# A residual block in one pipeline: the late order from body 3 on, and other PSUM banks

## The chip, the cores and the metric

The kernel runs on one core of a Trainium2 chip. The metric is the device time of one execution in microseconds (us); the table below has the median of three runs.

## What is computed

```python
def _L0_ffn_ref(x, Win, bin_, W1, b1, W2, b2, Wout, bout):
    s = jnp.einsum('btd,dm->btm', x, Win) + bin_
    h = jax.nn.relu(s[..., None] * W1 + b1)
    g = jnp.einsum('btmh,mh->btm', h, W2) + b2
    out = jnp.einsum('btm,md->btd', g, Wout) + bout
    return out
x = L0_attn_x                 # (4, 4096, 512), fp32
xn = _layernorm(x, axis=-1)
x = x + _L0_attn_ref(xn, ...) + _L0_ffn_ref(xn, ...)
```

The feed-forward part has 64 inner columns (M) with 16 hidden units each. The attention part runs only over 16 tokens of each of the 4 batches: it is three rounds of a small attention (a local linear map, layer norms, logits, softmax, product with the values) whose result picks, by a threshold, the output of the second or the third round, followed by Wo. Its result is added to those 64 rows of the output, all others get the bias bo alone.

## The kernel before, in words

The 16,384 rows of x are cut into 16 **pairs** (bodies) of 1,024 rows, two halves of 512. Each row is 2 KB, so a body loads 2.1 MB (`load`, `load_pair`) and stores as much; the second half is also read a second time in 32-row pieces (`load_quads`, 0.5 MB for each half of it, buffers `xq`, 1 MB a body), because VectorE turns it by stream transposes. That is 5.24 MB of DMA a body. For body n the steps are:

- TensorE turns the first half of x (`transpose` or `transpose_late`, into PSUM), ScalarE copies it out (`evacuate`, `evacuate_late`); VectorE turns the second half (`turn_quads`).
- VectorE takes statistics (`statistics`, eight of them, and `variance`), GpSimd makes 1/std (`inv_std`), TensorE spreads it over columns (`spread_rstd`, `spread_late`), ScalarE copies that into `s_full` (`copy_rstd`).
- TensorE multiplies by Win (`s_product`), VectorE scales (`scale_s`), and s is split into a high and a low part (`s_high` on ScalarE, `s_low` on VectorE).
- TensorE replicates s to the 1,024 hidden rows in two halves (`replicate`, banks `rep`), ScalarE does eight activations (`relu`), TensorE sums them with W2 in four steps (`sum_h`), ScalarE copies g out (`evacuate_g`), and TensorE multiplies by Wout in four pieces (`project`). VectorE adds each piece to x in place (`add`), GpSimd adds the bias (`add_bias`, eight), and SyncE stores.

Three bodies are in work at once: in iteration n of the main loops stand the first steps of body n, `replicate`, `sum_h` and the hidden activations of bodies n-1 and n-2, and `project` and `add` of body n-3. Every engine runs a program of its own, written out in order, with semaphores between them, and nothing reorders it. There are two loops. For n below LATE (10) the turned half goes through one bank in four groups of 128x128 tiles, each copied by 512 columns. From LATE on, `transpose_late` turns by 64x64 tiles into both TA banks, two chunks of columns, each copied by 1,024, and `s_product_late` uses 128x32 tiles. The loop below LATE has places (`reach(side, n, k)`) at which the attention's steps are slipped in; where each goes is set by the tables AT_PE, AT_ACT, AT_DVE and AT_POOL (32 n + place). In the loop from LATE on there are none, and the attention has to be over by then, since it works in the second TA bank (`A_ps`).

TensorE is used in tile shapes (rows x columns of the array): 128x128, 128x64, 128x32, 64x128 and 64x64. In the trace `project` is L628 (64x128), `replicate` L572 (64x128), `sum_h` L590 (128x32), `transpose` L474 (128x128), `transpose_late` and `spread_late` L482 (64x64), `s_product` L542 (128x64), `s_product_late` L518 (128x32). L329 (`product_qk`) and L356 are of the attention's setup: L356 turns the four weight matrices and ScalarE and VectorE (L997) copy them out; L329 waits for the copies of Wq and Wk.

The work of SyncE's queue at the start is one list of loads: x of bodies 0 and 1, biases, Wq, Wk, x of body 2, Wv, Wo, the quads of body 2, Wout and some 18 small loads, then x of body 3, for whose place Wq and Wk must have been turned.

## Time and profile before

| | us |
|---|---|
| median of 3 runs (lowest to highest) | 321.81 (321.6 to 322.66) |
| the profiled execution itself | 323.47 |
| its span | 321.7 |
| TensorE busy | 287.7 (89%) |
| VectorE busy | 251.5 (78%) |
| GpSimd busy | 236.5 (74%) |
| ScalarE busy | 232.8 (72%) |
| packets of SyncE's queue, share of 16 DMA engines | 67.3% |
| packets of ScalarE's queue, share of 16 DMA engines | 18.5% |

The span is what the trace shows from the first to the last instruction; 1.8 us of the profiled execution lie around it. An engine's busy time is a union over stages with different limits: read it by stretch. Every fp32 matmul stands in the trace as two records, and records of matmuls that run side by side in different tiles, or one behind the other in the pipeline, overlap; what a step costs TensorE is the distance from its first record to the first record of the next step.

### The profile page before, as it was taken

The numbers are of one execution on the slowest core, as the hardware profiler recorded it, in microseconds if no ns is written. First come the engines' busy times: TensorE is split into PE (matmuls) and PEld (weight loads), VectorE is DVE, ScalarE is ACT, GpSimd is POOL, SyncE is SP. The second block draws the span as 40 slices with busy tenths as digits, with TensorE's granted clock in tenths as the row PEclk, the third lists the DMA queues.
The fourth block names the chain that finished last, engine by engine and source line by source line (L and its number), as shares of the span: only waits on it lengthen the run. The fifth ranks groups of instructions, "written<-read, shape, count | busy, mean of one in ns | idle before, by whom it ended". The sixth has DMA issues, their size and how long they took to land.

```text
span 321.7 us, 5598 instructions
## 1 busy us (share of the span) xinstructions
PE 287.7 (89%) x2035; PEld 128.7 (40%) x2035; DVE 251.5 (78%) x400; ACT 232.8 (72%) x296; POOL 236.5 (74%) x209
## 2 busy tenths in 40 slices
PE   4878769989989999999999979899987999999882
PEld 3645514544533544345443424334332444342220
DVE  0769455679689787897889999999996899976444
ACT  1448624685896879987698776888868789898840
POOL 8440995781892989829895694598989498999960
PEclk9999969999999999999999999999997999999998
DMA  7999939996429979698996989899999999632697
GB/s 230 293 368 407 264 52 317 384 268 202 154 72 336 287 239 349 180 334 244 340 281 212 339 229 342 243 341 291 300 331 341 378 333 341 236 154 109 242 284 276
DMA packets 50571, 87.83 MB, mean 273 GB/s; under 512 B 6360, under 2 KB 35184, under 8 KB 46448
## 3 DMA queue, kind: packets, MB, share of 16 engines
q1 hardware_dynamic: 46400, 65.96, 67.3%
q10 hardware_dynamic: 3504, 21.37, 18.5%
q0 software_dynamic: 640, 0.16, 0.8%
q8 instruction: 16, 0.26, 0.4%
q14 instruction: 11, 0.09, 0.1%
HBM read 53.77 MB, written 33.69 MB: 272 GB/s over the span
## 4 chain that ended last, share of the span: by engine, by line
PE 45%; DVE 25%; SPq 9%; issue 8%; DMA 7%; ACT 2%; POOL 2%; ACTq 0%; DVEq 0%; POOLq 0%
PE op L628 9%; PE sg L590 9%; DVE x L1099 8%; DVE stats L1126 5%; PE sg L518 5%; SPq L245 4%; PE sg L542 4%; DMA out_dram<-x 4%; DMA xq<-in_L_attn_x_dram 3%; DVE xqT L1109 3%; PE rep L572 3%; SPq L264 3%; DVE SL L1120 3%; PE TA L329 2%; PE TA L474 2%
## 5 line engine op out<-in xcount | busy, mean ns | idle before, releaser
L1245 POOL TENSOR_TENSOR x<-x,bias_row 128x512 f32<-128x512 f32 x128 | 162.4, 1313 | 0.0
L840 ACT ACTIVATE H<-rep,b1c,w1c 128x1024 f32<-128x1024 f32 x124 | 143.7, 1219 | 18.2 <-PE rep L572 16.3
L1126 DVE BATCH_NORM_STATS2 stats<-x 128x6 f32<-128x512 f32 x128 | 79.7, 676 | 9.6 <-DMA x<-in_L_attn_x_dram 9.6
L1099 DVE TENSOR_TENSOR x<-x,op 128x1024 f32<-128x1024 f32 x53 | 64.3, 1213 | 19.8 <-PE op L628 19.7
L1229 POOL TENSOR_TENSOR rstd<-veps,nhalf 128x8 f32<-128x8 f32 x16 | 26.7, 1672 | 53.9 <-DVE veps L1136 53.9
L590 PE MATMUL sg<-H,w2s 128*32 128x512 f32 x512 | 64.2, 606 | 0.0
L628 PE MATMUL op<-wout,G 64*128 64x512 f32 x212 | 57.8, 622 | 4.9 <-DVE x L1099 4.1
L1109 DVE STREAM_TRANSPOSE xqT<-xq 128x1024 f32<-128x1024 f32 x28 | 34.6, 1235 | 10.1 <-PE sg L542 6.3
L542 PE MATMUL sg<-xT,win 128*64 128x512 f32 x80 | 36.4, 598 | 1.6 <-ACT xqT L804 1.6
L804 ACT ACTIVATE xT<-TA 128x512 f32<-128x512 f32 x40 | 24.0, 607 | 14.9 <-PE TA L474 14.8
L474 PE MATMUL TA<-ident,x 128*128 128x128 f32 x192 | 30.2, 290 | 3.9 <-DMA x<-in_L_attn_x_dram 2.6
L542 PE MATMUL sg<-xqT,winq 128*64 128x512 f32 x64 | 29.2, 598 | 0.0
L474 PEld LDWEIGHTS TA<-ident,x 128*128 128x128 f32 x192 | 22.2, 147 | 16.6 <-issue 9.6
L590 PEld LDWEIGHTS sg<-H,w2s 128*32 128x32 f32 x512 | 13.2, 108 | 33.6 <-issue 21.5
L628 PEld LDWEIGHTS op<-wout,G 64*128 64x128 f32 x212 | 17.3, 185 | 18.7 <-issue 10.5
L518 PE MATMUL sg<-xT,win 128*32 128x512 f32 x96 | 22.6, 614 | 0.0
L518 PE MATMUL sg<-xqT,winq 128*32 128x512 f32 x96 | 22.6, 614 | 0.0
L572 PE MATMUL rep<-SH,spread 64*128 64x512 f32 x62 | 17.9, 572 | 2.4 <-DVE SL L1120 2.3
L542 PEld LDWEIGHTS sg<-xT,win 128*64 128x64 f32 x80 | 10.1, 136 | 23.5 <-issue 23.5
L1231 POOL TENSOR_TENSOR rwide<-rstd,ones_d 128x512 f32<-128x512 f32 x16 | 17.0, 1062 | 1.3
L1114 DVE TENSOR_TENSOR s_full<-sg,s_full 128x512 f32<-128x512 f32 x16 | 10.8, 678 | 7.1 <-PE sg L518 7.1
L1120 DVE TENSOR_TENSOR SL<-s_full,SH 128x512 fp32r<-128x512 f32 x16 | 14.5, 908 | 1.8 <-ACT SH L826 1.8
(189 smaller groups left out, 363.0 us busy)
## 6 DMA issues: line engine op xcount, KB each, us to landing
out_dram<-x SPq DMA_DIRECT2D x30, 1024.0 KB, 6.0
x<-in_L_attn_x_dram ACTq DMA_DIRECT2D x10, 2048.0 KB, 11.2
xq<-in_L_attn_x_dram SPq DMA_DIRECT2D x112, 128.0 KB, 8.6
x<-in_L_attn_x_dram SPq DMA_DIRECT2D x12, 1024.0 KB, 12.2
out_dram<-x SPq DMA_DIRECT2D x4, 512.0 KB, 3.4
x<-in_L_attn_Wq_dram SPq DMA_DIRECT2D x1, 1024.0 KB, 18.8
x<-in_L_attn_Wk_dram SPq DMA_DIRECT2D x1, 1024.0 KB, 21.0
x<-in_L_attn_Wv_dram SPq DMA_DIRECT2D x1, 1024.0 KB, 16.1
```

The source lines that it names most:

```text
L474: mm = pe.transpose(bank(n, g)[:, j::TILES], x_sb[m][:, col0:col0 + P], ident[:, :])
L518: mm = pe.matmul(own, w[:, c, a * MH:(a + 1) * MH], turned_x, start=(c == 0), stop=(c == DC - 1))
L542: mm = pe.matmul(own, w[:, c, :], turned_x, start=(c == 0), stop=(c == DC - 1))
L572: mm = pe.matmul(rep_banks(n, half)[:, b * BLK:(b + 1) * BLK], spread[own, half, :], part[own, :], start=(part is SH), stop=(part is SL), ...
L590: mm = pe.matmul(g_ps[at0:at0 + MH, :], w2s[:, half, k, :], Hr[half][k % len(Hr[half])][:, b * BLK:(b + 1) * BLK], start=(k == 0), stop=(k ...
L628: mm = pe.matmul(sum_banks(n, j)[:, b * D:(b + 1) * D], G[n % 2][own, j * P:(j + 1) * P], wout[own, :], start=True, stop=True, tile_positi ...
L840: act.activation(Hr[half][k % len(Hr[half])][:, :], rep_banks(n, half)[:, :], ACT.Relu, bias=b1c[:, half, k:k + 1], scale=w1c[:, half, k:k ...
L1099: dve.tensor_tensor(both, both, sum_banks(n, j)[:, :].rearrange("p (h d) -> p h d", h=2), ALU.add).then_inc(add_done, 1)
L1109: dve.transpose(xqT[:, h * QH:(h + 1) * QH, :, :].rearrange("p t c a -> p (t c a)"), xq[k % 3][:, :]).then_inc(tq_done, 1)
L1126: dve.bn_stats(stats[:, j, :], x_sb[m][:, j * D:(j + 1) * D]).then_inc(bn_done, 1)
L1229: pool.tensor_tensor(rstd[:, :], veps[:, :], nhalf[:, 0:TPP], ALU.pow).then_inc(rstd_done, 1)
L1245: pool.tensor_tensor(x_sb[m][:, c], x_sb[m][:, c], bias_row[:, :], ALU.add).then_inc(xc_done, 1)
```

## The change

The second shape of the loop now serves bodies 3 to 15 (LATE is 3), in a new order on TensorE, ScalarE and VectorE, and has places for the attention. The eight PSUM banks are dealt anew: the attention gets a bank (`A`), g gets one, and s shares the second TA bank with the transposes, `spread_late` and piece 1 of `project`, which needs both. So of body n, TA holds in turn: s(n-1), piece 1 of body n-3, the two chunks of x, the spread, s(n). All eight statistics of a body are taken in the body before. The quads of body 2 are loaded ahead of Wv and Wo. The last bodies' order (the tail) is new. The tables of places are new from body 3 on, and equal ahead of it but for VectorE's statistics. Left out of the diff are the tables, the waits of `replicate` and `project` that follow from the banks, and `turn_halves`, which takes its target as an argument.

```diff
-        TA_ps, sg_ps, o_ps, rep_ps = ps("TA", 2), ps("sg", 2), ps("op", 2), ps("rep", 2)
-        T_ps, A_ps = TA_ps[:, 0:BLK], TA_ps[:, BLK:2 * BLK]
-        s_ps, g_ps = sg_ps[:, 0:BLK], sg_ps[:, BLK:2 * BLK]
+        TA_ps, g_ps, A_ps, o_ps, rep_ps = ps("TA", 2), ps("g"), ps("A"), ps("op", 2), ps("rep", 2)
...
-        LATE = 10
+        LATE = 3
...
         def early(n):
 
-            return 2 if n < LATE - 2 else min(TPP, 2 * (n - LATE + 4))
+            return 2 if n < LATE else TPP
...
             load_weight(1, Wk)
             load(2, 0)
             load(2, 1)
+            load_quads(0)
+            load_quads(1)
             load_weight(2, Wv)
             load_weight(3, Wo)
-            load_quads(0)
-            load_quads(1)
...
             if i == 0:
                 pe.wait_ge(*(landed(n, 0)))
-                pe.wait_ge(R_done, n)
-                if n == LATE:
-                    pe.wait_ge(att_made, 1)
+                pe.wait_ge(add_done, TILES * (n - 3) + 2)
...
         def s_product_late(n):
 
-            pe.wait_ge(s_done, n)
-            pe.wait_ge(ev_done, groups(n + 1))
+            pe.wait_ge(R_done, n + 1)
             pe.wait_ge(tq_done, 2 * (n + 1 - BY_PE))
...
-                if LATE - 3 < n < N - 2:
-                    pe.wait_ge(add_done, TILES * (n - 1) + 2)
...
         def sum_banks(n, j):
 
-            if LATE - 3 <= n < N - 3 and j == 1:
-                return sg_ps
-            if (n, j) in ((N - 3, 1), (N - 2, 1), (N - 2, 3), (LAST, 2)):
+            if n < N - 3 and j == 1:
                 return TA_ps
-            return rep_ps if (n, j) == (LAST, 1) else o_ps
+            if (n, j) in ((N - 2, 1), (N - 2, 3), (LAST, 2)):
+                return TA_ps
...
             for n in range(LATE, N):
+                replicate(n - 2, 1)
+                reach(side, n, 0)
                 project(n - 3, 0)
-                replicate(n - 2, 1)
+                reach(side, n, 1)
                 project(n - 3, 1)
+                reach(side, n, 2)
+                sum_h(n - 2, 0)
+                reach(side, n, 3)
+                sum_h(n - 2, 1)
+                reach(side, n, 4)
+                project(n - 3, 2)
+                reach(side, n, 5)
                 transpose_late(n, 0)
-                project(n - 3, 2)
-                sum_h(n - 2, 0)
-                sum_h(n - 2, 1)
+                reach(side, n, 6)
+                replicate(n - 1, 0)
+                reach(side, n, 7)
+                transpose_late(n, 1)
+                reach(side, n, 8)
+                project(n - 3, 3)
+                reach(side, n, 9)
+                spread_late(n)
+                reach(side, n, 10)
                 sum_h(n - 2, 2)
-                transpose_late(n, 1)
-                replicate(n - 1, 0)
-                project(n - 3, 3)
-                spread_late(n)
+                reach(side, n, 11)
                 sum_h(n - 2, 3)
+                reach(side, n, 12)
                 s_product_late(n)
+                reach(side, n, 13)
             replicate(N - 2, 1)
             project(N - 3, 0)
+            sum_h(N - 2, 0)
             project(N - 3, 1)
-            sum_h(N - 2, 0)
+            replicate(LAST, 0)
+            sum_h(N - 2, 1)
+            sum_h(N - 2, 2)
             project(N - 3, 2)
-            sum_h(N - 2, 1)
-            replicate(LAST, 0)
-            sum_h(N - 2, 2)
             sum_h(N - 2, 3)
-            replicate(LAST, 1)
             project(N - 3, 3)
             project(N - 2, 0)
+            replicate(LAST, 1)
             project(N - 2, 1)
+            project(N - 2, 2)
             sum_h(LAST, 0)
-            project(N - 2, 2)
+            project(N - 2, 3)
             sum_h(LAST, 1)
-            project(N - 2, 3)
             sum_h(LAST, 2)
             sum_h(LAST, 3)
...
             for n in range(LATE, N):
                 relu(n - 2, 4)
+                reach(side, n, 0)
                 relu(n - 2, 5)
+                reach(side, n, 1)
+                s_high(n - 1)
+                reach(side, n, 2)
                 relu(n - 2, 6)
-                s_high(n - 1)
+                reach(side, n, 3)
+                relu(n - 2, 7)
+                reach(side, n, 4)
                 evacuate_late(n, 0)
-                relu(n - 2, 7)
-                if has(n + AHEAD):
+                reach(side, n, 5)
+                relu(n - 1, 0)
+                reach(side, n, 6)
+                evacuate_late(n, 1)
+                if n + AHEAD >= RING and has(n + AHEAD):
                     load_pair(n + AHEAD)
-                evacuate_late(n, 1)
-                relu(n - 1, 0)
+                reach(side, n, 7)
+                relu(n - 1, 1)
+                reach(side, n, 8)
                 copy_rstd_late(n)
-                relu(n - 1, 1)
+                reach(side, n, 9)
+                relu(n - 1, 2)
+                reach(side, n, 10)
+                relu(n - 1, 3)
+                reach(side, n, 11)
                 evacuate_g(n - 2)
-                relu(n - 1, 2)
-                relu(n - 1, 3)
+                reach(side, n, 12)
             relu(N - 2, 4)
             s_high(LAST)
             relu(N - 2, 5)
             relu(N - 2, 6)
             relu(N - 2, 7)
             relu(LAST, 0)
+            relu(LAST, 1)
             evacuate_g(N - 2)
-            for r in range(1, TPP):
+            for r in range(2, TPP):
                 relu(LAST, r)
...
             for n in range(LATE, N):
                 scale_s(n - 1)
+                reach(side, n, 0)
+                variance(n)
+                reach(side, n, 1)
+                turn_quads(n, 0)
+                reach(side, n, 2)
                 add(n - 3, 0)
+                reach(side, n, 3)
                 add(n - 3, 1)
-                variance(n)
+                reach(side, n, 4)
+                s_low(n - 1)
+                reach(side, n, 5)
                 add(n - 3, 2)
-                turn_quads(n, 0)
-                s_low(n - 1)
+                reach(side, n, 6)
                 turn_quads(n, 1)
+                reach(side, n, 7)
+                add(n - 3, 3)
+                reach(side, n, 8)
                 if has(n + 1):
-                    statistics(n + 1, 0)
-                add(n - 3, 3)
-                if has(n + 1):
-                    for j in range(1, TPP):
+                    for j in range(TPP):
                         statistics(n + 1, j)
+                        reach(side, n, 9 + j)
```

What this does to the order is shown at three places. The names: `rep` is the replicated s, `H` the hidden activations, `G` the summed g, `SH` and `SL` the parts of s, `op`, `sg`, `g`, `TA` and `A` are PSUM banks, `x` and `xT` the rows and their transpose, `xq` the quads. Line numbers differ between the two kernels: L572, L590, L628, L482 and L518 are L566, L582, L619, L481 and L514 in the changed one.

TensorE, one body of the late shape (n = 13), from behind one `s_product_late` on, before:

```order
L628 MATMUL op<-wout,G 128x512 x2
L572 MATMUL rep<-SH,spread 128x512 x2
L572 MATMUL rep<-SL,spread 128x512 x2
L628 MATMUL sg<-wout,G 128x512 x2
L482 MATMUL TA<-ident,x 128x64 x16
L628 MATMUL op<-wout,G 128x512 x2
L590 MATMUL sg<-H,w2s 32x512 x12
L482 MATMUL TA<-ident,x 128x64 x16
L572 MATMUL rep<-SH,spread 128x512 x2
L572 MATMUL rep<-SL,spread 128x512 x2
L628 MATMUL op<-wout,G 128x512 x2
L482 MATMUL TA<-ident,rwide 128x64 x8
```

and now:

```order
L566 MATMUL rep<-SH,spread 128x512 x2
L566 MATMUL rep<-SL,spread 128x512 x2
L619 MATMUL op<-wout,G 128x512 x2
L619 MATMUL TA<-wout,G 128x512 x2
L582 MATMUL g<-H,w2s 32x512 x8
L619 MATMUL op<-wout,G 128x512 x2
L481 MATMUL TA<-ident,x 128x64 x16
L566 MATMUL rep<-SH,spread 128x512 x2
L566 MATMUL rep<-SL,spread 128x512 x2
L481 MATMUL TA<-ident,x 128x64 x16
L619 MATMUL op<-wout,G 128x512 x2
L481 MATMUL TA<-ident,rwide 128x64 x8
```

Two of the four `sum_h` of the body (x8 for x12) now stand ahead of the first transposes, and the two others behind the spread; `replicate` of the new body stands between the two chunks of transposes.

TensorE in the middle of the attention (L419 and L427 before, L401 to L418 now, are steps of its second round). Before, body 6:

```order
L419 MATMUL TA<-ident,vn 128x128 x4
L474 MATMUL TA<-ident,x 128x128 x4
L628 MATMUL op<-wout,G 128x512 x2
L572 MATMUL rep<-SH,spread 128x512 x2
L572 MATMUL rep<-SL,spread 128x512 x2
L474 MATMUL TA<-ident,x 128x128 x4
L550 MATMUL sg<-ident,rwide 128x128 x4
L427 MATMUL TA<-WvT,qk 64x256 x4
L628 MATMUL op<-wout,G 128x512 x2
L590 MATMUL sg<-H,w2s 32x512 x4
L474 MATMUL TA<-ident,x 128x128 x4
L628 MATMUL op<-wout,G 128x512 x2
```

and now, body 5, from its first chunk of transposes:

```order
L481 MATMUL TA<-ident,x 128x64 x16
L401 MATMUL A<-kT,bd 128x256
L402 MATMUL A<-vT,bd 128x256
L566 MATMUL rep<-SH,spread 128x512 x2
L566 MATMUL rep<-SL,spread 128x512 x2
L407 MATMUL A<-avg,vn 128x4 x4
L481 MATMUL TA<-ident,x 128x64 x16
L619 MATMUL op<-wout,G 128x512 x2
L412 MATMUL A<-ident,vT 128x128 x4
L481 MATMUL TA<-ident,rwide 128x64 x8
L582 MATMUL g<-H,w2s 32x512 x8
L418 MATMUL A<-ident,vn 128x128 x4
```

Four steps of a round stand in one body, between steps of other tile shapes, and the last of them (L418) directly ahead of the product with Win.

SyncE's queue at the start, before:

```order
L245 DMA x<-in_L_attn_x_dram 128x2048 x2
L267 DMA x<-in_L_attn_Wv_dram 128x4x512
L267 DMA x<-in_L_attn_Wo_dram 128x4x512
L264 DMA xq<-in_L_attn_x_dram 32x8x128 x8
L295 DMA wout<-in_L_ffn_Wout_dram 64x512
```

and now:

```order
L244 DMA x<-in_L_attn_x_dram 128x2048 x2
L263 DMA xq<-in_L_attn_x_dram 32x8x128 x8
L266 DMA x<-in_L_attn_Wv_dram 128x4x512
L266 DMA x<-in_L_attn_Wo_dram 128x4x512
L294 DMA wout<-in_L_ffn_Wout_dram 64x512
```

The eight quad loads of body 2 (1 MB) went ahead of Wv and Wo (2.1 MB).

## Rows read from the trace of the kernel before

**Rows 1.** Chain that ended last, 25 to 66 us (start, us, engine and line).
```profile
30.78 10.28 DMA xq<-in_L_attn_x_dram
...
42.96 6.67 PE TA L329 x16
```

**Rows 2.** VectorE in order of time, before L329.
```profile
41.09 1.25 DVE L1109 STREAM_TRANSPOSE xqT<-xq 128x1024 f32<-128x1024 f32 x1 [3.73 <-DMA xq<-in_L_attn_x_dram]
```

**Rows 3.** By stretch: us; busy PE, PEld, DVE, ACT, POOL; clock; DMA share; GB/s.
```profile
38.90:42.96 4.06, 0.05 (x1) 0.00 (x0) 1.87 (x3) 3.41 (x5) 4.06 (x5) 0.91 0.80 158
42.96:49.60 6.64, 6.64 (x17) 1.75 (x17) 2.29 (x3) 0.00 (x0) 6.64 (x6) 0.54 0.31 31
49.60:62.00 12.40, 12.40 (x100) 6.69 (x100) 8.61 (x20) 6.69 (x12) 6.60 (x6) 1.00 1.05 364
62.00:213.70 151.70, 144.51 (x950) 64.28 (x952) 131.49 (x211) 122.01 (x168) 110.77 (x85) 1.00 0.87 263
122.40:139.56 17.16, 16.78 (x106) 6.91 (x105) 14.54 (x20) 15.78 (x24) 13.28 (x11) 1.00 0.85 252
122.40:159.88 37.48, 36.84 (x239) 16.52 (x237) 31.62 (x49) 31.48 (x46) 29.18 (x23) 1.00 0.91 281
213.70:227.70 14.00, 13.61 (x132) 5.54 (x128) 13.86 (x21) 12.44 (x14) 13.04 (x11) 1.00 1.06 303
227.70:245.06 17.36, 14.57 (x133) 5.58 (x129) 17.22 (x27) 12.79 (x14) 16.43 (x14) 0.96 1.06 328
213.70:288.00 74.30, 69.93 (x648) 28.27 (x644) 69.10 (x100) 62.15 (x66) 65.34 (x51) 0.98 0.95 308
```

**Rows 4.** TensorE in order of time, body 6, four-group shape with attention.
```profile
126.00 0.66 PE L419 MATMUL TA<-ident,vn 128*128 128x128 f32 x4
126.50 0.60 PE L474 MATMUL TA<-ident,x 128*128 128x128 f32 x4
...
130.03 1.08 PE L427 MATMUL TA<-WvT,qk 128*64 128x256 f32 x8 [0.38 <-DVE qk L1057]
131.04 1.13 PE L628 MATMUL op<-wout,G 64*128 64x512 f32 x4
```

**Rows 5.** TensorE in order of time, body 11, late shape.
```profile
219.68 0.66 PE L482 MATMUL TA<-ident,x 64*128 64x64 f32 x16
220.18 1.08 PE L628 MATMUL op<-wout,G 64*128 64x512 f32 x4
221.27 2.78 PE L590 MATMUL sg<-H,w2s 128*32 128x512 f32 x24
...
225.07 0.49 PE L572 MATMUL rep<-SH,spread 64*128 64x512 f32 x2 [0.38 <-DVE SL L1120]
...
225.64 1.02 PE L628 MATMUL op<-wout,G 64*128 64x512 f32 x4
226.49 0.41 PE L482 MATMUL TA<-ident,rwide 64*128 64x64 f32 x8
226.83 1.07 PE L590 MATMUL sg<-H,w2s 128*32 128x512 f32 x8
...
231.26 1.13 PE L628 MATMUL op<-wout,G 64*128 64x512 f32 x4
```

**Rows 6.** ScalarE in order of time, body 11, late shape.
```profile
218.88 3.40 ACT L840 ACTIVATE H<-rep,b1c,w1c 128x1024 f32<-128x1024 f32 x3 [1.49 <-PE rep L572]
222.17 0.63 ACT L826 ACTIVATE SH<-s_full 128x512 fp32r<-128x512 f32 x1
222.69 1.02 ACT L815 ACTIVATE xT<-TA 128x1024 f32<-128x1024 f32 x1
```

**Rows 7.** DMA issues by kind (KB each, median us to landing).
```profile
x<-in_L_attn_x_dram SPq DMA_DIRECT2D x12, 1024.0 KB, 12.2
```

**Rows 8.** SyncE's queue in order of time, loads of body 3.
```profile
45.92 0.91 SPq L245 DMA_DIRECT2D x<-in_L_attn_x_dram  x2
```

**Rows 9.** Chain that ended last, 205 to 262 us, a store.
```profile
227.96 13.39 DMA out_dram<-x
```

45 lines of the change are left out of this document (22 added, 23 removed).

## The prediction

> **What bounds the kernel now.** I read the page's busy shares first, then busy time by stretch, then the chain that ended last, and for each place on which that chain rests the engine's instructions in order of time. Between the start of s(2) at 62.0 us and that of s(10) at 213.7 us, the eight bodies 3 to 10, TensorE is busy 144.51 of 151.70 us and no other engine over 131.5 [rows 3]; a pair of attention bodies takes 37.48 us with TensorE busy 36.84 [rows 3]. So TensorE's instruction stream sets the pace there. The five late bodies, 213.7 to 288.0, take 74.30 us with TensorE busy 69.93; an undisturbed one takes 14.00 us, with VectorE (13.86), GpSimd (13.04) and ScalarE (12.44) close behind, and the DMA engines full (share 1.06) [rows 3]. The start is another matter: the chain goes through the landing of the first quads (30.78 + 10.28 us) into L329, which takes 6.67 us [rows 1]; ahead of it TensorE did nothing for 4.06 us, and then worked at a granted clock of 0.54, near the lower of its two levels, 1.2 GHz [rows 3].
>
> **The start (quads ahead of Wv and Wo).** VectorE's queue stands behind the quads: it waits 3.73 us for them until 41.09 [rows 2], then copies the last turned part of Wk, and L329 waits for that copy. [...] At the 303 to 328 GB/s of full stretches [rows 3], 2.1 MB are over 6 us, more than the 3.73 us that VectorE waited. So L329 starts about 3.7 us sooner, and TensorE's gap of 4.06 us shrinks to some 0.3. The clock fell in that gap; without it the 6.64 us [rows 3] should shrink to half, 3.4, which gives 3.2 more. Bounds: 3.5 (the clock falls all the same) and 6.9. I take 6.9. From 49.6 to 62.0 TensorE is full, 12.40 of 12.40 us [rows 3], so all of it arrives. Against it: all eight statistics of body 3 now stand on VectorE ahead of the scaling of s(2). Body 3's x is issued at 45.92 [rows 8], and this kind lands 12.2 us later in the median [rows 7], so near 58; four statistics behind it end near 60, where s(2) would end at 58.7. I charge 1.0 us (bounds 0 and 3). **Start: -5.9.**
>
> **Bodies 3 to 10, TensorE's own work.** What does a body of the old shape cost without attention? Body 6 takes 17.16 us [rows 3]; off go L419, 0.50 us to the next step, and L427 with its wait, 0.38 + 1.01 [rows 4]. That leaves 15.27. A late body: 14.00 less the wait of 0.38 on SL [rows 3, 5] is 13.62. The new order has the same instructions. Its pieces, by start-to-start distances [rows 5]: `replicate` 0.57, `project` 0.85 where a 64x64 piece follows and 1.09 where `sum_h` does, `sum_h` 0.87 to 0.90, a chunk of transposes 0.50, the spread 0.34, s 3.56. In the new sequence: 0.66 + 0.85 + 1.09 + 1.90 + 0.95 + 0.50 + 0.57 + 0.50 + 0.85 + 0.34 + 1.77 + 3.56 = 13.5; I take 13.6. So each of bodies 3 to 9 loses 15.27 - 13.6 = 1.67 us of TensorE's work, 11.7 in all, and body 10 nothing. With the waits as long as now (151.70 - 144.51 = 7.2 us), bodies 3 to 10 would take 140.0.
>
> Changes of tile shape are the catch. The trace shows that one costs: `project` ahead of `sum_h` is 0.24 us dearer than ahead of a spread [rows 5]. The new body has nine changes, the late body before eight, the old shape eleven; I put one at 0.1 to 0.24. The Trainium skill, TensorEngine Tiling (Array Packing), Key Properties, states the general rule, which speaks against the hops: changing the tiling mode drains TensorE. By it every attention step (128x128) set between 64x64 pieces costs two drains; at the trace's 0.24 for each of some thirty extra changes that is up to 7 us, at 0.1 it is 3. Those are in the range, the smaller one in the walk below.
>
> **The waits of the new order.** I walked a pure late body. After s, `replicate` (0.57, and 0.2 that I allow until ScalarE starts), then on ScalarE four activations at 1.10, the high part at 0.52 [rows 6]. TensorE reaches the first chunk of transposes at 5.45 and ends it at 6.2, where ScalarE would have been ready at 5.7. Copy 1.02, one tenth, second chunk 0.7; between the copies ScalarE does the next body's first activation; second copy 1.02; so the spread can start at 9.35, while TensorE's own work ahead of it is 7.9. After it come 0.34 + 1.77 + 3.56. A pure body takes 15.0 us, not 14.0: TensorE waits some 0.5 us ahead of the second chunk and 0.7 ahead of the spread, with nothing to put there. In bodies 3 to 9 there is: L397, L401 and L407 stand in just these holes. Walking them with ScalarE's, VectorE's and GpSimd's steps I get 19.5, 16.9, 20.3, 16.2, 19.3, 15.8, 15.9 and 16.7 us for bodies 3 to 10, together 140.6; the worst places are L418 in bodies 5 and 7, which stands directly ahead of s and waits about 1 us for ScalarE's two copies and GpSimd's power for the layer norm. That agrees with the 140.0 above. Bounds: no waits at all, 133; nothing gained, 151.7. **Bodies 3 to 10: -11.1.**
>
> **Bodies 11 to 15.** 5 x 15.0 = 75.0 against 74.30: +0.7. The DMA: a body moves 5.24 MB; in 15.0 us that is 349 GB/s, and the full stretches show 303 to 328 [rows 3]. Before, a store took 13.39 us to land [rows 9], ScalarE stood before the next load of x, and body 12 took 17.36 instead of 14.00. Slower bodies ask for less, but bodies 3 to 10 leave less slack before them. I add 1.5 (bounds -3 and +6). **+2.2.**
>
> **The tail.** The same instructions with two changes of shape fewer, 2 x 0.24; piece 1 of body 13 goes to its own bank and waits for the add ahead of it, but `sum_h` covers that. **-0.5** (bounds +1 and -2).
>
> **Sum.** -5.9 - 11.1 + 2.2 - 0.5 = -15.3 against the profiled execution's 323.47 gives 308.2. That execution is 1.66 above the median of the three runs, 321.81; against the median the same sum gives **306.5 us**.
>
> **The rivals.**
> *No waits.* The attention fills every hole: bodies 3 to 10 at 133 to 136, no DMA trouble: 298 to 302. For it: TensorE is now at 98% in a pair. Against it: L418's place.
> *Other engines take the gain.* TensorE's saved time in bodies 3 to 10 turns into waits for ScalarE and GpSimd, because x, the spread and s of one body pass through the same two banks one after the other: only start and tail remain, with the +2.2, 317.6. For it: ScalarE is busy 84% of a pair, VectorE as much. Against: before, TensorE waited 0.64 us in 37.48, and ScalarE has 3 us of room a body [rows 3]. The Trainium skill, TensorEngine Tiling (Array Packing), PSUM Bottleneck, would have it so: tiling speeds up TensorE but not the copies out of PSUM, which may bind then. By that rule the time is this rival's; the trace leaves it its 0.11.
> *The DMA binds.* The pair at share 0.91 in 37.48 us needs 34 us of all 16 engines; in 35 it would be at 0.97. If stores land late as at 227.96 us three times more, each costs what it cost body 12, 17.36 - 14.00 = 3.4: 316.7.
> *Slower.* The one mechanism: everything that touches TA is a serial chain, s 3.56, scale 0.9, piece 1 1.1, add 1.2, two chunks 1.4, two copies 2.1, spread 0.4, its copy 0.6 and nine handovers 0.9, 12.2 us. If the attention's steps all fall into it, a pair adds TensorE's 6.3, ScalarE's 31.48 - 24.88 = 6.6 and VectorE's 31.62 - 27.72 = 3.9 [rows 3], 8.4 a body: 20.6 for each of bodies 3 to 9 and 15.0 for body 10, 159 instead of 151.7. With start, late bodies and tail that is +3.1: 325. It decides once an attention body takes over 20.1 us on average. Against it: four queues rarely line up so.
> *It doesn't do what it says.* The quads land no sooner, since they are many small packets and the whole list is DMA-bound: +5.9, about 312.
>
> **How the numbers follow.** Forecast with its own spread (303 to 313, the quads' case in it) 0.60; no waits 0.10; other engines 0.11; DMA 0.11; slower 0.08. The likeliest gives 306.5. The range goes from 299 (most of no waits) to 318 (other engines, DMA); outside lie the slower case and a little at either end. About 0.3% (1 us) can be told from no change here. Faster: 0.60 + 0.10 + 0.11 + 0.08 of the DMA's = 0.89; within 0.3%: 0.03; slower: 0.08.
>
> **What would show it.** Right: L329 in about 3.4 us from near 39.3 with the clock at 1.00 and no wait of VectorE for quads; s(2) near 55; bodies 3 to 10 in about 140 us with TensorE busy some 133; pure late bodies of 15.0 with waits ahead of the second chunk and the spread; L418 with a wait in bodies 5 and 7. Wrong: pairs still near 37.5 us with TensorE at 90%, pure bodies over 16, several stores of over 10 us with ScalarE standing before a load, or VectorE standing before the statistics of body 3 for over 2 us.

## The result, and the profile after

The changed kernel takes **314.01 us** (median of 4 executions; the kernel before 321.76, median of 4): ratio 0.9746, 95% interval 0.9716 to 0.9775. One of its four executions took 320.96 us and is left out of the ratio, though not of the median; the last experiments bear on how that can be. The time lies in the range (299 to 318), 7.5 us above the forecast of 306.5 and above the spread of 303 to 313 that the forecast was given for itself. The profiled execution took 314.29 us, its span is 312.5; it stands against the profiled 323.47 with its span of 321.7.

The first matmul of s of each block on TensorE cuts the trace into bodies (body n ends where s of block n starts):

| body | before, us | walked in the prediction | changed, us |
|---|---|---|---|
| start, up to s(2) | 61.94 | (-6.9) | 54.30 |
| 3 | 21.50 | 19.5 + 1.0 | 23.35 |
| 4 | 18.69 | 16.9 | 18.12 |
| 5 | 20.29 | 20.3 | 22.38 |
| 6 | 17.14 | 16.2 | 17.53 |
| 7 | 20.32 | 19.3 | 19.25 |
| 8 | 17.14 | 15.8 | 16.23 |
| 9 | 20.95 | 15.9 | 16.56 |
| 10 | 15.73 | 16.7 | 17.88 |
| 3 to 10 | 151.76 | 140.6 + 1.0 | 151.30 |
| 11 to 15 | 74.28 | 75.0 + 1.5 | 74.31 |
| rest of the span | 33.7 | (-0.5) | 32.6 |

So the start gave 7.6 us and the tail 1.1. The eight bodies to which the prediction gave the larger part of the gain gave 0.5. The stretches that answer to [rows 3], in the changed kernel, with the same columns (length; busy time and instructions of PE, PEld, DVE, ACT and POOL; clock; DMA share; GB/s). They are body 3, bodies 4 to 10, bodies 11 to 15, and 3 to 10:

```profile
54.30:77.65 23.35, 20.19 (x147) 9.88 (x147) 21.51 (x42) 16.82 (x21) 15.22 (x13) 1.00 0.93 307
77.65:205.60 127.95, 117.80 (x1055) 49.37 (x1058) 117.57 (x174) 105.83 (x134) 105.29 (x77) 1.00 0.85 267
205.60:279.91 74.31, 69.67 (x644) 26.70 (x640) 68.53 (x98) 62.75 (x67) 65.39 (x51) 1.00 0.95 313
54.30:205.60 151.30, 137.99 (x1201) 59.24 (x1204) 139.08 (x215) 122.65 (x155) 120.50 (x90) 1.00 0.87 274
```

In bodies 3 to 10 TensorE's work did fall, from 144.6 to 138.0 us, but its idle time rose from 7.2 to 13.3. VectorE is now the busiest engine there (139.1 us, 131.5 before). On the page's chain of work that ended last, over the whole span, TensorE's share fell from 45% to 41% and VectorE's rose from 25% to 29% (before, then changed):

```profile
PE 45%; DVE 25%; SPq 9%; issue 8%; DMA 7%; ACT 2%; POOL 2%; ACTq 0%; DVEq 0%; POOLq 0%
PE 41%; DVE 29%; issue 10%; DMA 8%; ACT 7%; POOL 3%; ACTq 1%; DVEq 0%; POOLq 0%
```

At the start, what [rows 1, 2] showed is gone. The product of q and k (L328, L329 before) takes 3.65 us for 6.67, and TensorE waits 0.30 us ahead of it. Behind that stand body 3's first waits (TensorE in order of time):

```profile
38.34 3.65 PE L328 MATMUL A<-x,xnT 128*64 128x512 f32 x16 [0.30 <-DVE x L1016]
...
59.47 0.44 PE L377 MATMUL A<-ident,vn 128*128 128x128 f32 x2 [1.52 <-DVE kT L1033]
...
66.61 0.71 PE L387 MATMUL A<-centre,qkn 128*128 128x128 f32 x4 [1.40 <-DVE qkn L1045]
```

VectorE in body 3 and at the head of body 4:

```profile
53.92 4.84 DVE L1145 BATCH_NORM_STATS2 stats<-x 128x6 f32<-128x512 f32 x8
58.68 0.41 DVE L1032 TENSOR_TENSOR qT<-A,bqs 128x256 f32<-128x256 f32 x1
61.08 0.69 DVE L1133 TENSOR_TENSOR s_full<-TA,s_full 128x512 f32<-128x512 f32 x1 [1.67 <-ACT s_full L815]
63.92 2.63 DVE L1045 TENSOR_TENSOR qkn<-repw,block 128x128 f32<-128x128 f32 x3
...
82.21 0.16 DVE L1151 SCALAR_TENSOR_TENSOR m<-stats 128x8 f32<-128x8 f32 x1
82.32 1.22 DVE L1153 SCALAR_TENSOR_TENSOR dm<-dmean 128x8 f32<-128x8 f32 x1
83.57 1.19 DVE L1155 SCALAR_TENSOR_TENSOR veps<-m,dm 128x8 f32<-128x8 f32 x1
```

All eight statistics of block 3 stand ahead of qT and kT, so L377 waits 1.52 us. And two of the variance's four operations over 8 columns take 1.2 us each in body 4, where the one ahead of them takes 0.16. Beside them GpSimd does three bias additions without a pause:

```profile
80.98 3.76 POOL L1272 TENSOR_TENSOR x<-x,bias_row 128x512 f32<-128x512 f32 x3
84.84 1.65 POOL L1256 TENSOR_TENSOR rstd<-veps,nhalf 128x8 f32<-128x8 f32 x1
```

The Trainium skill, SBUF — State Buffer, Who interferes with whom, states that a VectorE instruction with two inputs in SBUF contends with a GpSimd instruction that reads SBUF, and that one of them then stands. The trace agrees in part: all four operations of the variance have two such inputs; two of them take 1.2 us in body 4 (the others 0.32 and 0.16), and none over 0.17 in body 3. In the order before, the variance was never slowed: its four operations had means of 165 to 167 ns in the same bodies, against 162, 300, 425 and 429 now. Other operations of VectorE were, there too (L1057, a scaling of 128x256, took 817 ns on average, and 351 in a run below that takes GpSimd's work away).

### The profile page after: what moved, and what is told of

Read it like the earlier page. It is cut to its first block, busy times and chain, and to the rows that moved or that the text cites. A ratio compares the mean times of both kernels' runs of the same rounds, so it can differ in the third digit from the quotient of the medians.

```text
span 312.5 us, 6071 instructions
## 1 busy us (share of the span) xinstructions
PE 279.0 (89%) x2287; PEld 123.2 (39%) x2287; DVE 259.3 (83%) x400; ACT 232.5 (74%) x282; POOL 241.0 (77%) x209
## 3 DMA queue, kind: packets, MB, share of 16 engines
q10 hardware_dynamic: 3504, 21.37, 19.6%
## 4 chain that ended last, share of the span: by engine, by line
PE 41%; DVE 29%; issue 10%; DMA 8%; ACT 7%; POOL 3%; ACTq 1%; DVEq 0%; POOLq 0%
PE TA L514 10%; PE g L582 10%; DVE stats L1145 8%; DVE x L1118 8%; PE op L619 6%; DMA out_dram<-x 5%; ACT xT L820 3%; DMA b2c<-in_L_ffn_b_dram 3%; PE TA L481 3%; ACT H L845 3%; PE rep L566 2%; PE TA L619 2%; DVE xqT L1128 2%; DVE SL L1139 2%; PE A L328 1%
## 5 line engine op out<-in xcount | busy, mean ns | idle before, releaser
L845 ACT ACTIVATE H<-rep,b1c,w1c 128x1024 f32<-128x1024 f32 x124 | 144.4, 1206 | 24.2 <-PE rep L566 21.9
L582 PE MATMUL g<-H,w2s 128*32 128x512 f32 x512 | 62.6, 599 | 0.4 <-ACT H L845 0.4
L619 PE MATMUL op<-wout,G 64*128 64x512 f32 x184 | 49.9, 620 | 1.2 <-ACT G L852 0.8
L514 PE MATMUL TA<-xT,win 128*32 128x512 f32 x208 | 47.0, 593 | 0.3 <-ACT s_full L825 0.3
L514 PE MATMUL TA<-xqT,winq 128*32 128x512 f32 x208 | 47.0, 593 | 0.0
L820 ACT ACTIVATE xT<-TA 128x1024 f32<-128x1024 f32 x26 | 26.7, 1025 | 8.2 <-PE TA L481 7.7
L582 PEld LDWEIGHTS g<-H,w2s 128*32 128x32 f32 x512 | 12.8, 108 | 29.8 <-issue 14.6
L514 PEld LDWEIGHTS TA<-xT,win 128*32 128x32 f32 x208 | 12.1, 110 | 29.8 <-issue 25.9
L481 PEld LDWEIGHTS TA<-ident,x 64*128 64x128 f32 x416 | 15.9, 139 | 15.7 <-issue 8.3
L619 PEld LDWEIGHTS op<-wout,G 64*128 64x128 f32 x184 | 14.9, 186 | 17.3 <-DVE x L1118 10.0
L481 PE MATMUL TA<-ident,x 64*128 64x64 f32 x416 | 18.0, 226 | 3.7 <-ACT xT L820 3.0
L1118 DVE TENSOR_TENSOR x<-x,TA 128x1024 f32<-128x1024 f32 x16 | 19.3, 1209 | 1.3 <-PE TA L619 1.3
L619 PE MATMUL TA<-wout,G 64*128 64x512 f32 x64 | 16.9, 605 | 0.6 <-DVE s_full L1133 0.6
L566 PE MATMUL rep<-SH,spread 64*128 64x512 f32 x62 | 15.4, 494 | 1.7 <-DVE SL L1139 1.3
```

The lines of the kernel that those rows point to most:

```text
L481: mm = pe.transpose(to[:, h, j::TILES], tile(j)[own, :], ident[own, own], tile_position=(h * M, 0))
L514: mm = pe.matmul(own, w[:, c, a * MH:(a + 1) * MH], turned_x, start=(c == 0), stop=(c == DC - 1))
L582: mm = pe.matmul(g_ps[at0:at0 + MH, :], w2s[:, half, k, :], Hr[half][k % len(Hr[half])][:, b * BLK:(b + 1) * BLK], start=(k == 0), stop=(k ...
L619: mm = pe.matmul(sum_banks(n, j)[:, b * D:(b + 1) * D], G[n % 2][own, j * P:(j + 1) * P], wout[own, :], start=True, stop=True, tile_positi ...
L820: act.activation(xT[:, 2 * i:2 * i + 2, :].rearrange("p c (h x) -> p h c x", h=2), half_banks, ACT.Copy).then_inc(ev_done, 1)
L845: act.activation(Hr[half][k % len(Hr[half])][:, :], rep_banks(n, half)[:, :], ACT.Relu, bias=b1c[:, half, k:k + 1], scale=w1c[:, half, k:k ...
```

## The experiments

Theory A: the order gave nothing in bodies 3 to 10 because VectorE, slowed by GpSimd at the head of the bodies, takes what TensorE saves. Rivals: TensorE's saving was never as large as computed (C); GpSimd's own queue is the one that is late (A4); the steps of attention, which pass over four engines, run at their own pace.

### The two halves of the change apart

```diff
+            load_quads(0)
+            load_quads(1)
             load_weight(2, Wv)
             load_weight(3, Wo)
-            load_quads(0)
-            load_quads(1)
```

This alone, on the kernel before:

> The kernel before, and of the change only the order of the loads: the quads of x of block 2 ahead of Wv and Wo. Theory A (the whole gain comes from the start, and the order of bodies 3 to 10 gave none): the first s product of block 2 moves from 61.94 to about 54.3 us, bodies 3 to 10 stay at 151.8, and the time is 321.8 - 7.6 = 314.2 us, within 0.5 us of the changed kernel. Rival (the early load needs the new order, or bodies 3 to 10 take the gain back, as their waits on VectorE are set by something that is not earlier): 317 to 321 us.

**Measured: 318.15 us** (ratio 0.9906, 0.9873 to 0.9939), the rival's figure. s(2) starts at 54.65, but body 3 takes 24.98 us for 21.50; bodies 4 to 10 are as before, 11 to 15 take 72.86 us for 74.28. TensorE and VectorE in it:

```profile
66.12 0.71 PE L388 MATMUL TA<-centre,qkn 128*128 128x128 f32 x4 [3.00 <-DVE qkn L1026]
```

```profile
62.24 3.82 DVE L1026 TENSOR_TENSOR qkn<-repw,block 128x128 f32<-128x128 f32 x3
```

The early start meets a row of GpSimd's additions: three two-input operations of 128 columns take 3.82 us (1.95 in the kernel before, 0.70 in runs below, where GpSimd left room). TensorE's wait there is 3.00 us for 1.13, and its granted clock over body 3 is 0.93 for 1.00, with 1.6 us more of busy time (21.98 for 20.37). The forecast of 314.2 was wrong, since it took the start's gain to arrive whole; body 3 gives 3.5 us of it back.

The opposite, the changed kernel with the loads as before (the same lines swapped back):

> The changed kernel with the loads in the order of before. Theory A: the start loses its 7.6 us and the rest stays, so 314.0 + 7.6 = 321.6 us, no difference from the kernel before. Rival (the new order of bodies 3 to 10 has a gain of its own that hangs on nothing at the start): 316 to 319 us.

**Measured: 318.62 us** (0.9906, 0.9877 to 0.9936), the rival's figure. s(2) starts at 61.35, body 3 takes 21.76, bodies 3 to 10 take 149.68, the rest as in the changed kernel. So the order does have a gain of its own, 3.2 us by the medians, of which 2.1 lie in bodies 3 to 10; the loads give 3.7 alone and 4.6 on top of the order. Moving them up brings the start 7.1 us forward and costs body 3 1.6 of it (23.35 - 21.76).

### The place of the variance and of the statistics

```diff
             scale_s(n - 1)
-            variance(n)
             turn_quads(n, 0)
             add(n - 3, 0)
             add(n - 3, 1)
+            variance(n)
             s_low(n - 1)
```

> The changed kernel with the variance of block n behind add 1 of block n-3 on VectorE, its place in the order of before, where add 0 and add 1 stood ahead of it. Theory A1 (the four small operations of the variance, slowed to some 1.2 us each beside GpSimd, stand in the chain from scale_s over add 1 to the first transposes, which share banks with that sum): bodies 4, 5 and 7 get 1 to 2 us shorter each, 3 to 6 us in all, 308 to 311 us. Rival A2 (the chain runs through what VectorE does for attention and the late variance only moves the wait to the spread, at the body's end): within 1 us of 314.0. Rival A3: the reciprocal deviations come too late for the spread in the bodies without attention and every body gets longer by about 1 us: 320 us or more.

**Measured: 321.48 us** (0.9990, 0.9959 to 1.0022), slower than the changed kernel by 7.5 us. Bodies 3, 4 and 5 are shorter by 1.7, 0.5 and 0.2 us, where A1 had 1 to 2 us for each of 4, 5 and 7, and bodies 6, 7 and 8 take 19.23, 21.15 and 22.39 us (17.53, 19.25, 16.23 in the changed kernel). None of the three readings had that. Bodies 11 to 15 stay at 14.75, so A3's mechanism is out. The chain of body 8:

```profile
163.86 2.26 DVE x L1118 x2
...
166.43 0.18 DVE veps L1155
...
166.68 2.03 POOL rstd L1256
...
168.79 1.06 POOL rwide L1258
169.84 1.01 POOL WvT L1250
...
170.88 0.02 ACT WvT L792
```

GpSimd's queue is in order: the power waits for the late variance, and behind the power stands L1250, attention's subtraction, for which ScalarE and with it the transposes wait. The wait that I moved away from VectorE's head came back through GpSimd. In that body TensorE's granted clock was 0.85, so part of its 6.2 us may be the clock. The chain is shown for body 8; that 6 and 7 lose in the same way is argued from it. The gain of body 3 has a cause of its own: its variance was not slowed in the changed kernel (0.17 us each), but with the variance late GpSimd starts its power at 67.21 us instead of 62.33, and VectorE's three operations of L1045, at 63.7, run beside an idle GpSimd in 0.69 us instead of 2.63.

The same cut on body 3 alone, statistics too:

```diff
     def early(n):
-        return 2 if n < LATE else TPP
+        return 2 if n <= LATE else TPP
...
             turn_quads(n, 1)
+            if n == LATE:
+                for j in range(2, TPP):
+                    statistics(n, j)
+                variance(n)
```

(the variance at its new place from body 4 on, and `inv_std(3)` behind six bias additions instead of one)

> The changed kernel, with six of the eight statistics of block 3, and its variance, put back into body 3 behind the second half of the quads; bodies 4 to 15 as changed. Theory A: body 3 (23.35 us in the changed kernel, 21.50 before) gets shorter by 1.5 to 3 us, as qT and kT are no longer behind 4.8 us of statistics, and the time is 311 to 312.5 us. Rival (body 3 is set by the chain of attention and its hops between the engines, which goes on behind the statistics at its own pace): under 0.5 us, 313.5 to 314.5 us.

**Measured: 323.71 us** (1.0081, 1.0050 to 1.0113); body 3 takes 32.12 us, the others as changed. Its chain:

```profile
74.65 3.55 DVE stats L1145 x6
...
78.63 0.18 DVE veps L1155
...
78.88 1.66 POOL rstd L1261
...
80.60 1.07 POOL rwide L1263
...
81.72 0.69 PE TA L481 x8
82.41 1.15 PE A L401 x2
```

Now the spread waits for the statistics, and attention's L401 behind it on TensorE's queue. In the changed kernel the spread starts at 73.41. The early statistics and variance are what lets the spread go so soon; their 1.5 us ahead of L377 are the smaller price. The longer row of bias additions plays no part: GpSimd's power starts 0.07 us behind the variance. My expectation had charged the statistics with the whole excess of body 3.

### Bodies without attention

Both kernels return from the side work of each engine ahead of the three rounds; the choice and the projection behind them are left out as well.

```diff
             .then_inc(bqk_ps, 1)
+            return
             for it in range(ROUNDS):
```

> The changed kernel without the three rounds of attention and without the choice and projection behind them (the first rows of the output lack them); the bodies 3 to 10 then hold the main work alone, in the four shapes. Theory A (attention and VectorE's load around it make the new order's bodies long): bodies 4 to 10 run at 14.8 us like the bodies 11 to 15, bodies 3 to 10 take 118 to 121 us instead of 151.3, and the time is 281 to 284 us. Theory C (TensorE pays for the shapes themselves there, whatever attention does): the same 118 to 121 us, but then the same kernel before, also bare, differs from it by far less than the 11.7 us that the prediction computed.

> The kernel before without the three rounds of attention and what follows them, as in the run beside it: bodies 3 to 9 in the old form. The prediction computed that a bare body in the new form is 1.5 us shorter. Theory A: bodies 3 to 10 take 129 to 133 us, 10 to 13 us more than in the changed kernel's bare run, so that the saving is there once attention is gone and is eaten only beside it. Theory C: no more than 5 us above the changed kernel's bare run, so that the saving on TensorE was mostly not there to begin with.

**Measured: 289.63 us** (0.9005, 0.8975 to 0.9035) and **298.62 us** (0.9268, 0.9225 to 0.9310). The bodies 4 to 10, first of the changed kernel, then of the one before:

```profile
75.19:180.90 105.71, 97.95 (x900) 37.18 (x896) 99.64 (x144) 87.83 (x92) 90.59 (x70) 1.00 1.01 323
```

```profile
79.53:189.32 109.79, 106.01 (x670) 41.94 (x672) 101.17 (x149) 89.48 (x105) 90.31 (x70) 1.00 1.00 314
```

Seven bare bodies are 4.1 us shorter in the new order. Bodies 3 to 10 take 126.4 us against 129.2, within theory C's bound of 5 us, and A's 10 to 13 falls. But the time can't decide between them: by the prediction's own walk a bare body takes 15.0 us for 15.27, so theory A should never have had 10 to 13. TensorE's busy time can. One of the seven, body 10, had the late shape before as well. The six that changed their shape, 4 to 9, keep TensorE busy for 15.27 us each before (91.64 in all), just as computed, and 14.01 now (84.03), where I computed 13.6: a saving of 1.27 for 1.67. Body 3 saves 0.36 (17.40 and 17.04). It is the first body of the new shape and holds two spreads, the one of block 2, 0.5 us, and its own; where the rest of its shortfall goes is open. Body 10 saves 0.45. All eight save 8.4 us (123.4 less 115.0) of the 11.7 computed, **so part of the saving was never there.** In the new order a bare body waits 1.1 us (105.71 less 97.95, by seven); the walk had 1.4. That leaves it to attention to fill these holes. It added 20.5 us to bodies 4 to 10 before (130.26 less 109.79) and adds 22.2 now (127.95 less 105.71); the walk had 16.1 (121.1 less 105.0). TensorE's own part of it rose too, from 18.2 to 19.9 us, for the same steps.

### GpSimd's bias additions over 8 columns

```diff
-            c = slice(j * D, (j + 1) * D)
-            pool.tensor_tensor(x_sb[m][:, c], x_sb[m][:, c], bias_row[:, :], ALU.add)
+            c = slice(j * D, j * D + 8)
+            pool.tensor_tensor(x_sb[m][:, c], x_sb[m][:, c], bias_row[:, 0:8], ALU.add)
```

> The changed kernel with each of GpSimd's bias additions over 8 of its 512 columns (the rest of the bias is left out), which takes most of GpSimd's work away and leaves its order. Theory A1 (VectorE's small operations are slowed by GpSimd's work beside them): the operations of the variance fall from 1.2 to 0.2 us, VectorE's busy time in bodies 3 to 10 falls by 6 us or more, and the time by 4 to 8 us, to 306 to 310 us. Rival (the waits of bodies 3 to 10 come from the chain of attention's steps over four engines): the small operations get short, and the time stays within 1.5 us of 314.0.

> The kernel before with the same short bias additions. Theory A1: VectorE is less of a limit there, and the time falls by less than in the changed kernel, by 0 to 2 us, to about 320 to 321.8 us. Rival (GpSimd slows VectorE alike in both orders): both fall by the same amount within 1 us.

**Measured: 305.87 us** (0.9522, 0.9485 to 0.9559), 8.1 below the changed kernel, and **318.35 us** (0.9903, 0.9879 to 0.9927), 3.4 below the kernel before. Bodies 3 to 10 take 143.77 and 148.27 us. The 3.4 lie outside both readings for the kernel before: more than A1's 0 to 2 us, and not alike in both orders. In the changed kernel with short additions (body 3, then 4 to 10):

```profile
54.03:74.74 20.71, 20.08 (x148) 9.86 (x147) 18.15 (x39) 16.82 (x21) 4.46 (x8) 1.00 1.08 337
74.74:197.80 123.06, 117.08 (x1056) 49.51 (x1059) 107.25 (x174) 105.58 (x134) 40.70 (x79) 1.00 0.90 283
```

TensorE's work is the same (137.2 against 138.0 us) and its idle time 6.6 us for 13.3. The bodies are 20.71, 16.89, 20.65, 16.87, 19.23, 16.23, 16.55 and 16.64: five of the eight within 0.45 us of the walk, the others 0.65 to 1.2 above it. Together they take 143.8 us, where the walk and the 1.0 for the statistics give 141.6. **The walk was 2 us short for a VectorE and a GpSimd that leave each other alone, and it had not seen that they don't.** VectorE's groups in bodies 3 to 10, changed kernel:

```profile
L1139 DVE TENSOR_TENSOR SL<-s_full,SH 128x512 fp32r<-128x512 f32 x8 | 7.5, 941 | 0.0
L1153 DVE SCALAR_TENSOR_TENSOR dm<-dmean 128x8 f32<-128x8 f32 x8 | 3.4, 429 | 0.0
L1155 DVE SCALAR_TENSOR_TENSOR veps<-m,dm 128x8 f32<-128x8 f32 x8 | 3.4, 425 | 0.3
L1045 DVE TENSOR_TENSOR qkn<-repw,block 128x128 f32<-128x128 f32 x3 | 2.6, 929 | 0.0
L1109 DVE TENSOR_SCALAR xnT<-xnT,dsum 128x256 f32<-128x256 f32 x1 | 1.2, 1151 | 0.0
```

and with the short additions (over the same stretch, 54.3 to 205.6 us, which takes in a ninth variance, that of body 11):

```profile
L1139 DVE TENSOR_TENSOR SL<-s_full,SH 128x512 fp32r<-128x512 f32 x8 | 5.5, 687 | 0.0
L1153 DVE SCALAR_TENSOR_TENSOR dm<-dmean 128x8 f32<-128x8 f32 x9 | 1.5, 167 | 0.0
L1155 DVE SCALAR_TENSOR_TENSOR veps<-m,dm 128x8 f32<-128x8 f32 x9 | 1.5, 167 | 0.3
L1109 DVE TENSOR_SCALAR xnT<-xnT,dsum 128x256 f32<-128x256 f32 x1 | 0.4, 353 | 0.0
```

The four operations of the variance, 10.5 us before, take 5.2 in eight bodies. The statistics (675 and 679 ns) and the additions with an input in PSUM (1202 and 1211) don't change. These runs take two things away at once, the contention and the length of GpSimd's queue; the next ones part them to some degree.

### Versions that try to keep the gain

```diff
             scale_s(n - 1)
-            variance(n)
+            if n >= LATE + 3:
+                variance(n)
...
             add(n - 3, 1)
+            if n < LATE + 3:
+                variance(n)
```

> The changed kernel with the variance behind add 1 in bodies 3, 4 and 5 alone, where that place made the bodies 1.72, 0.53 and 0.16 us shorter in the run that had it in all bodies, and in its new place from body 6 on, where the late variance cost 1.7, 1.9 and 6.2 us (bodies 6 to 8). If what a body gains or loses hangs on its own variance: 2.4 us less than the changed kernel, 311.6 us, bodies 6 to 10 as in it. Rival (the 1.7 us of body 6 come from the late variance of body 5, which passes its delay on): 313.3 us.

**Measured:** six executions, 310.85, 310.99 and then 316.15, 316.37, 316.98 and 323.6. They part, so there is no ratio; the median is 316.26. In the profiled one (310.99) bodies 3 to 5 take 20.71, 17.55 and 22.22, and 6 to 10 are those of the changed kernel (17.52 for body 6): the first reading holds, a body hangs on its own variance. The whole, 316.26, met neither forecast. Body 3 gave more than the 1.72 us forecast: its end came at the same time as in the run with every variance late (75.66 and 75.85 us), but s(2) started 0.7 us later (54.95) and L377 waited 0.60 us for 1.53.

The variance off VectorE altogether, with bias additions whole:

```diff
+        def variance_gp(n):
+            pool.wait_ge(bn_done, ...)
+            (six tensor_tensor / tensor_scalar over 128x8 on GpSimd)
...
             if n >= LATE:
+                variance_gp(n)
                 inv_std(n)
```

(`variance(n)` is gone from VectorE's loop, and VectorE's statistics of the next block wait for GpSimd's variance.)

> The changed kernel with the variance of the blocks 3 to 15 computed by GpSimd, in six small operations ahead of its power, instead of VectorE's four; the bias additions stay whole. Theory A1 (what bodies 3 to 10 lose beside GpSimd, they lose by VectorE's small operations at the head of the body): VectorE's 10.5 us in the variance are gone, and 3 to 5 us of the 8.1 that the short bias additions gave come here too: 309 to 311 us. Rival A4 (they lose it in GpSimd's own queue, where the power and the subtraction of attention stand behind bias additions): six more operations in that queue, no gain or a loss, 314 to 318 us.

**Measured: 313.45 us** (median of six, two of them at 317.4 and 317.6; the ratio, 0.9717, 0.9676 to 0.9757, is that of the other four, at 312.5 to 314.0, and lies 0.9 us below the changed kernel's). Bodies 4 to 10 take 125.10 us for 127.95: with the bias additions whole, 2.85 us of the excess go with VectorE's small operations, so theory A1 has its share, less than its 309 to 311 us; A4 named no gain or a loss, and its figure of 314 to 318 us was near, but no loss came. The profiled execution was one of the long ones, and shows where they come from. VectorE, GpSimd, TensorE:

```profile
45.31 6.58 DVE L1140 TENSOR_TENSOR SL<-s_full,SH 128x512 fp32r<-128x512 f32 x1 [0.51 <-ACT SH L832]
```

```profile
38.95 12.39 POOL L1287 TENSOR_TENSOR x<-x,bias_row 128x512 f32<-128x512 f32 x10
```

```profile
53.73 1.97 PE L356 MATMUL op<-ident,x 128*128 128x128 f32 x8 [4.62 <-DVE WoT L1017]
```

One subtraction of 0.69 us stood through five of ten bias additions in a row, ended 0.5 us after the last of them (38.95 + 12.39 = 51.34), and TensorE stood 4.62 us; TensorE's granted clock was 0.63 from 50 to 55 us, 1.00 in the changed kernel. s(2) began at 60.58 instead of 54.3. So:

```diff
+                if n == 2:
+                    pool.wait_ge(sl_done, 2)
                 if has(n - 1):
                     add_bias(n - 1, 1)
```

> The kernel of the run with the variance late in bodies 3 to 5, and in body 2 GpSimd waits ahead of one of its ten bias additions in a row until VectorE's subtraction for the low part of s of block 1 is done. In one profiled execution that subtraction (two inputs, 0.69 us when alone) took 6.58 us beside that row of additions and TensorE then stood 4.6 us. If that is what parts the executions at 311 from those at 316 to 317: all of them near 310.9 (310 to 312), none over 313. Rival (the executions part for another reason, a chip's clock or DMA): still two groups some 5.5 us apart, median 311 to 316.

> The kernel beside it, and from body 4 on the variance on GpSimd; body 3 keeps it on VectorE behind add 1. Bodies 4 to 10 took 125.10 us with the variance on GpSimd and 127.18 in the run with it late on VectorE. If these gains add: 2.1 us less than the kernel beside it, 308.8 us (308 to 310). Rival (GpSimd's longer queue meets the shorter body 3 and gives it back): 310 to 312.

**Measured: 311.97 us** (0.9691, 0.9662 to 0.9719), all six between 311.10 and 312.89, where four of six had been above 316. That agrees with the reading, but the two runs were on different chips, and only one of the long executions was profiled: the lost time is shown for that one execution to come from the subtraction, for the others it is argued. The rival, that the chip or the DMA parts them, is not excluded. And **310.43 us** (0.9648, 0.9614 to 0.9682) with the variance of bodies 4 and up on GpSimd. In the first, VectorE and GpSimd:

```profile
46.63 0.69 DVE L1139 TENSOR_TENSOR SL<-s_full,SH 128x512 fp32r<-128x512 f32 x1 [0.51 <-ACT SH L831]
```

```profile
47.41 6.23 POOL L1275 TENSOR_TENSOR x<-x,bias_row 128x512 f32<-128x512 f32 x5 [0.89 <-DVE SL L1139]
```

The pause costs body 3 1.0 us (21.74 for 20.71): GpSimd's row ends later, two operations of block 2's variance now meet it (1.22 and 1.19 us), and the statistics of block 3 start at 54.84 instead of 53.65, so that L377 waits 1.64 us for 0.60. So the first figure lies 1.1 us above the one forecast, at the edge of its 310 to 312; the step from it to the second is 1.5 us where 2.1 were forecast. The last kernel is 3.6 us faster than the changed one, 11.3 us faster than the kernel before; its bodies 4 to 10:

```profile
75.88:201.64 125.76, 117.68 (x1056) 49.40 (x1059) 114.47 (x151) 105.83 (x134) 114.00 (x120) 1.00 0.88 279
```

One of its six executions still took 321.24 us. It was not profiled, so what happened in it stays open.

## Why the prediction was right or wrong, point by point

**The start, right.** L329's 3.4 us forecast, 3.65 measured, clock 1.00, no wait for quads; s(2) at 54.30 ("near 55"). The term was 6.9, the profiled executions show 7.6: the product starts 4.6 us sooner (3.7 forecast) and is 3.0 shorter (3.2). The 3.7 went by VectorE's wait for the quads, and loads of SyncE's queue do not strictly land in the order of their issue: before, Wo, issued at 19.0 us, landed 19.6 us later, and the first of the quads, issued at 21.9, 15.1 us later and so ahead of it. In the changed kernel VectorE turns its first quads at 36.37 us without a wait, where it had waited until 41.09. The profiled execution of the kernel before was 1.66 us above its median; where in it that lies is not known, and if all of it lay ahead of s(2), the term by the medians would be about 6.

**The statistics of body 3, charged with 1.0, bounds 0 and 3.** L377 waited 1.52 us for them. The right size, and not avoidable in that way: put back together with the variance, they cost 8.8.

**Bodies 3 to 10, the step that failed: -11.1 forecast (-10.1 with the statistics' 1.0, which fall into body 3), -0.5 measured.** It fails by two terms of like size (5.1 and 4.7 us), the saving of TensorE's work and the waits.
1. *TensorE's own work.* "Each of bodies 3 to 9 loses 1.67 us, 11.7 in all": its busy time fell by 6.6. Of the 5.1 missing, 2.4 are the piecewise sum of 13.6, 0.4 short of the measured 14.0 in each of bodies 4 to 9 (the 15.27 was exact); 1.3 are body 3, which the prediction took for a body like the others, and which holds one spread more; body 10, set at nothing, gave 0.45; and attention's steps cost TensorE 1.7 us more in bodies 4 to 10 than before and 0.2 more in body 3. The prediction had put 3 to 7 us on that in its range, by [rows 5], and 3 in the walk. The Trainium skill, TensorEngine Tiling (Array Packing), Key Properties, has a change of the tiling mode drain TensorE; the 1.7 us agree in sign, at 0.06 us for each of the thirty extra changes, less than the 0.1 to 0.24 of the prediction. No run varied the changes alone, so that the 1.7 come from them is not shown.
2. *The waits.* 7.6 us forecast (140.6 less 133), 8.6 with the statistics' 1.0, and 13.3 measured, 6.6 with short bias additions. The kernel before waited for VectorE alone (7.2 us; its three longest):

```profile
PE op L628 <- DVE x L1099: 2.6, 2, 1.4
PE TA L388 <- DVE qkn L1026: 1.1, 1, 1.1
PE sg L628 <- DVE s_full L1114: 1.0, 1, 1.0
```

The walk put ScalarE's copies in their place. They came (5.1 us, lines below), and VectorE's waits stayed (6.9 us in all). The prediction has no term for operations of VectorE that stand beside GpSimd's, and the new order put small two-input ones beside its additions. Of the 7.5 us that short additions gave back in these bodies (151.30 less 143.77), 2.85 hang on the variance of bodies 4 to 10 (gone with it on GpSimd), and 1.6 to 2.6 on body 3 (21.74 and 20.71 with its variance late, where L1045 took 0.70 in both). How the other 2 to 3 us part between the remaining slowed operations and GpSimd's queue is open.

**Bodies 11 to 15: +2.2 forecast, 0.0 measured.** A pure body did get longer, as the walk said: 14.75 us for 14.01 (15.0 forecast), with a wait of 0.23 us ahead of the second chunk and 0.47 ahead of the spread. The five come out even because the disturbed bodies did not recur: the longest takes 15.22, where body 12 had taken 17.35, and the term of 1.5 us for the DMA did not come. As bodies 3 to 10 did not get shorter, the queues were not pressed harder either; in the bare run, bodies 4 to 10, at DMA share 1.01 and 323 GB/s, took 15.1 us on average.

**The tail:** -0.5 forecast, -1.1 measured; no run looks into it.

**The rivals.** "Other engines take the gain" had named this outcome for bodies 3 to 10 (151.7, measured 151.30) and got a chance of 0.11. Its time of 317.6 was too high because it kept the +2.2 and a start of 5.9. Its mechanism, waits for ScalarE and GpSimd along one chain of banks, is in part the one that acted. TensorE waited 5.1 us in 11 places for ScalarE's copies in bodies 3 to 10,

```profile
PE TA L481 <- ACT xT L820: 5.1, 11, 0.8
PE A L397 <- DVE qT L1095: 1.7, 1, 1.7
PE A L377 <- DVE kT L1033: 1.5, 1, 1.5
PE A L387 <- DVE qkn L1045: 1.4, 1, 1.4
```

and for no copy of ScalarE's before: against the kernel before, the 6 us of new idle time are ScalarE's, as this rival says. Against the walk, which had them (0.5 a body and more), the excess is VectorE's: its waits of 1.4 to 1.7 us stand at three steps of attention, in bodies 3 and 5. L418, the walk's worst place, has no wait. Of the prediction's signs of being wrong, the first is half met: the pair of bodies 6 and 7 takes 36.8 us for 37.5 with TensorE busy 94%, and bodies 5 and 6 take 39.9 with 89%. The slower rival (bodies 3 to 9 over 20.1 us on average) did not come near: 19.1. That the time lies in the range is no credit to the forecast's mechanism: the range's upper end, 318, was drawn for the other rivals. The late bodies, the tail and the start erred by 3.5 us in the kernel's favour, which is luck and offset a third of the 9.6 missing in bodies 3 to 10; without it, 317.5 would still have been inside.

## What to carry to other kernels

Before an order is walked, mark on VectorE's queue every operation with two SBUF inputs and lay GpSimd's row of work beside it: only if GpSimd pauses there is its duration sure to be that of the alone case (128x8 operations took 0.16 to 1.2 us here). A long unbroken row on GpSimd is a hazard even where it has slack: one small operation behind it cost 6 us in one execution, and a wait that makes GpSimd yield there cost 1 us. A step that looks cheap to delay (a variance, statistics) must be followed through every in-order queue behind it: a late variance cost 7.5 us, late statistics and variance of one body 9.7. And a saving on the busiest engine is best measured bare first, by its busy time: 8.4 us of the computed 11.7 were there.

## What was not expected of the hardware

- A 128x512 subtraction of 0.69 us took 6.58 us beside GpSimd's additions: it did not get in between two of them, but only when the row of ten had ended. The Trainium skill, SBUF — State Buffer, Who interferes with whom, says of VectorE's two-port modes that whoever issues first holds the shared ports for its whole instruction and the other is fully blocked. Here, with a subtraction of two SBUF inputs, it was five instructions.
- In six other profiled executions with the early quads the same subtraction meets a row of whole additions and takes 0.7 to 1.7 us. Three of them, the changed kernel and the two runs with a late variance, run the same program up to that point as the one with 6.58 us, so which case comes is not decided by the program alone.
- Also slowed beside GpSimd: a multiplication by a per-partition scalar with one tensor input (L1109, 1151 ns against 353 with the short additions).
